# An adjacency pass that adds up in PSUM: pair sums in five banks, copied out by ScalarE, with the weighted one-hots as bf16 thirds from VectorE

## The chip, the cores and the metric

The kernel runs on one core of one Trainium2 chip. The metric is the device time of one execution in microseconds, lower is better; three runs of the kernel before gave a median of 9933.13 us (9930.52 to 9941.49).

## The reference, cut to what matters

Four graph layers over the same graph of 3125 nodes with 48 features and 100000 edges. The change touches how the graph itself is brought into a form that the layers read. The two middle layers are powers of an adjacency matrix, once counted and once weighted:

```
m = segment_sum(w[:, None] * h[row], col)        # layer 1: w from degrees, 5 steps
agg = segment_sum(f[src] * edge_weight[:, None], dst)   # layer 2: 10 steps
```

Layer 0 (attention, four rounds) and layer 3 (one message pass by relation) read sorted edge records and one-hot matrices.

## The kernel before, in words

**Sorting (`sort_edges`, L79 to L624).** Nodes are cut into 25 blocks of 128, so an edge belongs to one of 625 block pairs (source block, destination block). Edges are sorted by pair into tiles of 128 edges, one edge to a partition; each pair has at least one tile, and each source block's tiles are filled up to a multiple of four. There is room for T = 1488 tiles in NG = 372 groups of G = 4. With the inputs used here the 625 pairs need 1080 tiles (270 groups: 44 tiles for most source blocks); the last 102 groups hold no edge and are worked through all the same. A tile's record in DRAM (`REC`) has the numbers of its edge in columns CW to GIDX: cutoff, weight, norm, lane within the source block (SL), lane within the destination block (DL), index. They come from the tile `meta`, which VectorE fills at L272 to L291. The block ends with a loop (L354 to L368) that marks for every tile which pair it belongs to.

**Tables (`tile_tables`, L652 to L717).** VectorE alone works out, on one partition, where each tile's sum belongs (`row_at`), and whether a tile goes on with the pair of the tile ahead (`keep`).

**Adjacency (`adjacency`, L720 to L885).** For each tile a 128x128 matrix of counts and one of weights is made as a product of one-hot matrices, and added to the pair's place in `acc` (128 partitions, 2 x 50 x 128 numbers, two source blocks' rows). A group passes through:
- SyncE: loads the records (L769), and stores the turned one-hots to `OHT` in DRAM (L773), four groups later.
- VectorE: `hots` makes source one-hots and destination one-hots, two tiles at a time, four `tensor_tensor` in a group (L835); `rows` (L859) loads four numbers of `row_at` into registers; `add_up` (L869 to L881) adds each tile's two products into `acc`, one `scalar_tensor_tensor` of 128x256 a tile (L879), two groups behind. The order by hand is at L884: an addition between every two one-hot instructions.
- ScalarE: widens the source one-hots to fp32 (L786), scales the destination one-hots by the weight (L791, four in a group), copies the turned one-hots out of PSUM (L799).
- TensorE: eight transposes (L810, L811), four bf16 products (L820), four fp32 products (L822) in a group.
- GpSimd: clears `acc` at the start (L746), waits for the end of each source block, and sends its row of 3.2 MB to `ADJ` (L759).

The records, one-hots and semaphores have six slots (`laps(..., SLOTS)`), so a stage is at most five groups ahead of what frees its slot.

**After it** come the start of the nodes, gate and attention passes that read `OHT`, two `propagate` calls that read `ADJ` (their GpSimd queue also sends norm, lanes and index on to `REC2`), and the relation pass. Each stage ends in a barrier of all engines.

Of the kernel before, what the change touches and what calls it, by code (L numbers as in the profile page):

```python
# [42 lines left out]
CW, W, NORM, SL, DL, GIDX = 50, 51, 52, 53, 54, 55  # L43
GATES = 56
RW = GATES + H
META = GATES - CW
# [11 lines left out]
ROW = 2 * P * NB  # L58
HOT = 3
# [19 lines left out]
def sort_edges(nc, mem, io):  # L79
# [11 lines left out]
    with ExitStack() as ctx:  # L91
# [31 lines left out]
        turn = sb("turn", [EP, ET], F32)  # L123
# [11 lines left out]
        base = sb("base", [NB, NB], F32)  # L135
        earlier = sb("earlier", [NB, NB], F32)
        ones_n = sb("ones_n", [NB, P], BF16)
        iota_t = sb("iota_t", [NB, T], F16)
        ended = sb("ended", [NB, 2, T], BF16)
        fill2 = sb("fill2", [P, T2 // 8, META - 2], F32)  # L140
# [23 lines left out]
        s_pair = sem("s_pair")  # L164

# [8 lines left out]
        with nc.Block() as block:  # L174
            @block.sync
            def _(sp):
# [13 lines left out]
                sp.wait_ge(s_filled, 16 * (T // FR) + 128)  # L190

            @block.gpsimd
            def _(pool):
# [13 lines left out]
                nc.gpsimd.memset(fill2[:, :, DL - NORM:DL - NORM + 1], -1.0).then_inc(s_fill, 1)  # L207

            @block.scalar
            def _(act):  # L210
                act.wait_ge(s_turn, 1)
                nc.scalar.activation(sine, turn[:], ACT.Sin, scale=SIN_SCALE).then_inc(s_sine, 1)
# [50 lines left out]
            def _(dve):  # L263
# [18 lines left out]
                ch.step(v.tensor_scalar(turn[:], wt[:], 1.0 / 12, None, ALU.mult))  # L282
                ch.step(v.tensor_copy(tmp_i[:], turn[:]))
                ch.step(v.tensor_copy(sine, tmp_i[:]))
                ch.step(v.tensor_tensor(turn[:], turn[:], sine, ALU.subtract))
                v.tensor_scalar(turn[:], turn[:], -1.0, 1.0, ALU.max, ALU.min).then_inc(s_turn, 1)
                ch.step(v.tensor_copy(meta[:, :, W - CW], wt[:]))
                dve.wait_ge(s_sine, 1)
                ch.step(v.tensor_tensor(turn[:], sine, sine, ALU.mult))
                ch.step(v.tensor_scalar(sine, turn[:], -1.0, 1.0, ALU.mult, ALU.add))  # L290
                ch.step(v.scalar_tensor_tensor(meta[:, :, 0], wt[:], 6.0, sine, ALU.is_lt, ALU.mult))  # L291
                dve.wait_ge(s_const, 5)
# [43 lines left out]
                ch.step(v.tensor_scalar(ends[:], ends[:], before[:, 0:1], None, ALU.add))  # L336
                ch.step(v.tensor_tensor(base[:], ends[:], tiles[:], ALU.subtract))
# [87 lines left out]
        with nc.Block() as block:  # L425
# [120 lines left out]
            def _(dve):  # L546
# [22 lines left out]
                def ranks(n, slot, first):  # L569
# [6 lines left out]
                    v.tensor_copy(rec[:, slot, :, CW:GATES], meta[:, cols]).then_inc(s_meta, 1)  # L576
# [75 lines left out]
def tile_tables(nc, mem):  # L652


    for name, shape, dt in (("where", [1, NG * WHERE], I32), ("row_at", [1, NG * G], I32), ("spot", [1, T2], I32), ("goes_on", [P, NG], F32),
                            ("fresh", [P, NG], F32), ("last", [1, NB], I32)):
        mem[name] = nc.alloc_sbuf_tensor("m_" + name, shape, dt)
    with ExitStack() as ctx:
# [3 lines left out]
        odd = sb("odd", [1, T])  # L662
        odd_i = sb("odd_i", [1, T], I32)
# [13 lines left out]
        with nc.Block() as block:  # L677
            @block.vector
            def _(dve):
                v = nc.vector  # L680
                ch = Chain(dve, s_tab)
                ch.note(v.memset(mem["keep"][:, 0:1], 0.0))
                ch.note(v.tensor_tensor(mem["keep"][:, 1:T], mem["pair"][:, 1:T], mem["pair"][:, 0:T - 1],
                                        ALU.is_equal))


# [8 lines left out]
                ch.note(v.tensor_copy(odd_i[:], mem["sblk_t"][0:1, :]))  # L695
                ch.step(v.scalar_tensor_tensor(dblk[:], mem["sblk_t"][0:1, :], -float(NB), pair, ALU.mult, ALU.add))

                ch.note(v.tensor_scalar(sblk[:], mem["sblk_t"][0:1, :], 1.0, float(KEEP), ALU.max, ALU.mult))
                ch.step(v.tensor_scalar(odd_i[:], odd_i[:], 1, None, ALU.bitwise_and))
                ch.step(v.tensor_copy(odd[:], odd_i[:]))  # L700
                row_at = mem["row_at"][:].rearrange("o (g j) -> o g j", j=G)
                ch.step(v.scalar_tensor_tensor(odd[:], odd[:], float(NB), dblk[:], ALU.mult, ALU.add))
# [17 lines left out]
def adjacency(nc, mem):  # L720


    SLOTS = 6
    SUMS = 3
    with ExitStack() as ctx:
        room = Room(nc, ctx, "a_")
        rec = room.sb("rec", [P, SLOTS, G, META])
# [1596 lines left out]
```

## Time and profile before

| what | us |
|---|---|
| median of three runs | 9933.13 |
| span of the profiled execution | 10065.2 |
| sorting, 0 to 1490 | 1490 |
| tables, 1490 to 1536 | 46 |
| adjacency, 1536 to 2928 | 1392 |
| start of nodes and gate pass, 2928 to 3680 | 752 |
| attention, four rounds, 3680 to 7240 | 3560 |
| propagation, twice, 7240 to 8745 | 1505 |
| relation pass and end, 8745 to 10065 | 1320 |

The profiled execution is 132 us (1.3%) longer than the median of the runs without a profile. Over the whole span PE is busy 71%, VectorE (DVE) 60%, GpSimd (POOL) 47%, ScalarE (ACT) 37%. These averages mix stages with different limits; a row of a group of instructions gives its busy time, the mean duration of one, and the idle time of the engine ahead of it with what ended that idle time.

### The profile page before, as it was taken

The numbers are of one execution on the slowest core, as the hardware profiler recorded it, in microseconds if no ns is written. First come the engines' busy times: TensorE is split into PE (matmuls) and PEld (weight loads), VectorE is DVE, ScalarE is ACT, GpSimd is POOL, SyncE is SP. The second block draws the span as 40 slices with busy tenths as digits, with TensorE's granted clock in tenths as the row PEclk, the third lists the DMA queues.
The fourth block names the chain that finished last, engine by engine and source line by source line (L and its number), as shares of the span: only waits on it lengthen the run. The fifth ranks groups of instructions, "written<-read, shape, count | busy, mean of one in ns | idle before, by whom it ended". The sixth has DMA issues, their size and how long they took to land. (4 is left out here: it accounts for less than half of the span.)

```text
span 10065.2 us, 316920 instructions
## 1 busy us (share of the span) xinstructions
PE 7153.0 (71%) x106494; PEld 5756.9 (57%) x106495; DVE 6009.4 (60%) x18492; ACT 3716.3 (37%) x12956; POOL 4708.2 (47%) x6247
## 2 busy tenths in 40 slices
PE   2888865766657849976994998599578788833323
PEld 1555544555547749975994898499434344433323
DVE  6555558888867778997997899799700100011112
ACT  3222216777753326753662676377300000000000
POOL 0777770000016625542551554255267476556665
PEclk9999998888879979987996999799799899855555
DMA  8222224555439949965992997499488899611112
GB/s 330 60 61 61 62 52 162 192 186 188 136 103 308 310 137 255 263 178 147 261 261 65 262 263 205 121 262 263 128 333 334 322 365 364 236 29 18 18 18 19
DMA packets 1841808, 1846.73 MB, mean 183 GB/s; under 512 B 1462965, under 2 KB 1477717, under 8 KB 1796469
## 3 DMA queue, kind: packets, MB, share of 16 engines
q1 hardware_dynamic: 1727618, 1668.62, 54.0%
q0 software_dynamic: 112016, 153.10, 5.9%
q10 hardware_dynamic: 2016, 22.94, 0.6%
q8 instruction: 94, 1.54, 0.1%
q14 instruction: 64, 0.52, 0.0%
HBM read 1481.79 MB, written 360.62 MB: 183 GB/s over the span
## 5 line engine op out<-in xcount | busy, mean ns | idle before, releaser
L1649 POOL TENSOR_TENSOR s_rest<-s_msg 128x196 f32<-128x196 f32 x1488 | 762.6, 512 | 1881.7 <-ACT s_msg L1631 1819.4
L1239 PE MATMUL s_gotd<-m_table_d,s_hot 128*128 x17856 | 1363.2, 205 | 207.3 <-DMA s_hot<-OHT 195.2
L1631 ACT ACTIVATE s_msg<-s_gotd,s_es 128x49 f32<-128x49 f32 x5952 | 1304.4, 303 | 48.3 <-ACT s_es L1624 0.2
L1239 PE MATMUL s_gotq<-m_table_s,s_hot 128*128 x17856 | 1280.0, 185 | 7.1 <-issue 6.9
L1239 PEld LDWEIGHTS s_gotd<-m_table_d,s_hot 128*128 128x128 bf16 x17856 | 989.1, 96 | 291.4 <-DMA s_hot<-OHT 196.6
L1916 POOL DMA_INDIRECT REC<-m_sums x800 | 957.1, 1196 | 353.5 <-issue 346.8
L463 POOL DMA_INDIRECT REC<-rec,place x800 | 960.9, 1201 | 260.5 <-issue 228.5
L2195 POOL DMA_INDIRECT l_row<-H,l_rec x816 | 786.6, 964 | 501.3 <-issue 252.7
L1682 DVE TENSOR_REDUCE s_tops<-s_mt 128x512 f32 (+1 forms) x1488 | 1013.6, 681 | 6.5 <-PE s_mt L1592 6.3
L1949 PE MATMUL p_acc<-p_row,p_feats 128*64 128x512 f32 (+1 forms) x4032 | 900.2, 570 | 160.3 <-DMA p_row<-ADJ 157.3
L1239 PEld LDWEIGHTS s_gotq<-m_table_s,s_hot 128*128 128x128 bf16 x17856 | 992.1, 97 | 5.9 <-issue 5.9
L1253 PE MATMUL l_sums<-l_msg,l_oh 128*128 128x49 f32 x1632 | 373.4, 378 | 817.6 <-issue 798.2
L1253 PEld LDWEIGHTS l_sums<-l_msg,l_oh 128*128 128x128 f32 x1632 | 379.3, 321 | 813.1 <-issue 812.8
L1592 PE MATMUL s_mt<-m_ident_bf,s_raw 128*128 128x128 bf16 x5952 | 823.3, 219 | 4.3 <-issue 4.2
L1591 PE MATMUL s_mt<-s_hot,m_apart 128*128 128x128 bf16 x5952 | 823.0, 218 | 2.9 <-issue 1.7
L1656 POOL TENSOR_TENSOR s_least<-s_rest 128x196 bf16<-128x196 f32 x1488 | 762.9, 513 | 116.7
L1949 PEld LDWEIGHTS p_acc<-p_row,p_feats 128*64 128x64 f32 x4032 | 385.3, 140 | 654.1 <-issue 430.8
L879 DVE SCALAR_TENSOR_TENSOR a_acc<-a_acc,m_keep,a_sums 128x256 f32 x1488 | 706.1, 475 | 64.3 <-issue 49.4
L822 PE MATMUL a_sums<-a_hd_weighted,a_hs_wide 128*128 128x128 f32 x2976 | 662.0, 350 | 0.0
L1612 PE MATMUL s_sums<-s_msg,s_hot 128*128 128x49 bf16 x5952 | 621.0, 186 | 48.8 <-issue 41.1
L1612 PE MATMUL s_sums<-s_least,s_hot 128*128 128x49 bf16 x5952 | 620.6, 184 | 4.1 <-issue 4.1
L1612 PE MATMUL s_sums<-s_rest,s_hot 128*128 128x49 bf16 x5952 | 622.2, 186 | 1.7 <-issue 1.6
(422 smaller groups left out, 18333.1 us busy)
## 6 DMA issues: line engine op xcount, KB each, us to landing
s_hot<-OHT SPq DMA_DIRECT2D x1488, 384.0 KB
p_row<-ADJ SPq DMA_DIRECT2D x288, 1600.0 KB
s_rec<-REC SPq DMA_DIRECT2D x1488, 98.0 KB
OHT<-a_turned SPq DMA_DIRECT2D x372, 384.0 KB
g_hot<-OHT SPq DMA_DIRECT2D x372, 384.0 KB
ADJ<-a_acc POOLq DMA_DIRECT2D x25, 3200.0 KB
REC<-fill SPq DMA_DIRECT2D x124, 624.0 KB, 10.2
g_rec<-REC SPq DMA_DIRECT2D x372, 108.0 KB
```

The costliest lines, as they stand in the source:

```text
L463: nc.gpsimd.indirect_dma_start(out=mem["REC"], out_offset=bass.IndirectOffsetOnAxis(ap=place[:, b, j:j + 1], axis=0), in_=rec[:, b, j], in ...
L1239: last = nc.tensor.matmul(out, hot, table[k][:, bass.ds(at, w)], start=(k == 0), stop=(k == 2))
L1591: nc.tensor.matmul(mt[:, j], mem["apart"][:], hot[:, b, j, 1], start=True, stop=False)
L1592: last = nc.tensor.matmul(mt[:, j], upper(raw[:, b % KEPT, j:j + 1]).to_broadcast([P, P]), mem["ident_bf"][:], start=False, stop=True)
L1612: last = nc.tensor.matmul(sums[:, 0:SW], hot[:, b, j, 2], thirds[k], start=(j == 0 and k == 0), stop=(j == G - 1 and k == 2))
L1631: last = nc.scalar.activation(msg[:, b % KEPT, j], gotd[b % KEPT][:, j, SW:2 * SW], ACT.Copy, scale=es[:, b % 2, j:j + 1])
L1649: nc.gpsimd.tensor_tensor(rest[:, b % KEPT].rearrange("p g w -> p (g w)"), msg[:, b % KEPT].rearrange("p g w -> p (g w)"), upper(msg[:, b ...
L1656: nc.gpsimd.tensor_tensor(least[:, b % KEPT].rearrange("p g w -> p (g w)"), rest[:, b % KEPT].rearrange("p g w -> p (g w)"), upper(rest[:, ...
L1682: v.tensor_reduce(tops[:, bass.ds(n, 1)], mt[:].rearrange("p j e -> p (j e)"), X, ALU.max).then_inc(s_top, 1)
L1916: nc.gpsimd.indirect_dma_start(out=mem["REC2"], out_offset=bass.IndirectOffsetOnAxis(ap=places_of[b][:, t:t + 1], axis=0), in_=numbers_of[ ...
L1949: last = nc.tensor.matmul(acc[odd * SIDE:(odd + 1) * SIDE, q, 0:n * P].rearrange("w (c e) -> w c e", e=P), feats[:, s], source.rearrange(" ...
L2195: nc.gpsimd.indirect_dma_start(out=row[:, b, j], out_offset=None, in_=table, in_offset=bass.IndirectOffsetOnAxis(ap=rec[:, b, j, GIDX - NO ...
```

## The change

- `sort_edges`: `meta` has eight columns instead of six. The weight is stored as three numbers, each exact in bf16 (its bf16 value, the bf16 value of the rest, the rest of that); norm and index move behind DL, and the record in `REC` keeps its width. The running ends of the pairs' tiles are written to DRAM and loaded back onto one partition (`pair_end`) by SyncE. Some tiles share memory with others.
- `tile_tables`: `keep` and `row_at` go; `pair_at` comes, for each tile the start of its PSUM bank, and for a group's last tile also the number of its pair.
- `adjacency`: the counts and weights of a pair's tiles add up in one of five PSUM banks (pair k in bank k mod 5), both products of a tile in bf16: one matmul for the counts, three for the weight's thirds. ScalarE waits for the end of each pair by its number in `pair_end`, copies the bank's 256 columns into `acc`, waits for that, and writes zeros to the bank. It also starts the DMA of each row, which GpSimd did. VectorE makes all one-hots with one `tensor_scalar` a tile and kind: two for the plain ones, three for the weighted ones, with two scalars from the record each; it also copies the turned one-hots out of PSUM. `acc` needs no clearing and no addition.
- `propagate` and `relation_pass` take the columns at their new places.

```diff
@@ sort_edges
-                ch.step(v.tensor_copy(meta[:, :, W - CW], wt[:]))
...
+                third, less = tmp_i[:].bitcast(BF16)[:, 0:ET], turn
+                ch.step(v.tensor_copy(third, wt[:]))
+                ch.step(v.tensor_copy(meta[:, :, W - CW], third))
+                ch.step(v.tensor_tensor(less, wt[:], third, ALU.subtract))
+                ch.step(v.tensor_copy(third, less))
+                ch.step(v.tensor_copy(meta[:, :, W - CW + 1], third))
+                ch.step(v.tensor_tensor(meta[:, :, W - CW + 2], less, third, ALU.subtract))
...
+                v.tensor_copy(ends_i[:], ends[:]).then_inc(s_ends, 1)
...
+                sp.wait_ge(s_ends, 1)
+                sp.dma_start(mem["PAIR_END"].rearrange("(s d) -> s d", d=NB), ends_i[:]).then_inc(s_ends_out, 16)
+                sp.wait_ge(s_ends_out, 16)
+                sp.dma_start(mem["pair_end"][:], mem["PAIR_END"].rearrange("(o k) -> o k", o=1)).then_inc(s_ends_out, 16)
+                sp.wait_ge(s_ends_out, 32)
@@ tile_tables
+                fives = sblk[:]
+                ch.step(v.tensor_scalar(fives, dblk[:], float(BANKS), None, ALU.is_ge))
+                for k in range(2, NB // BANKS):
+                    ch.step(v.scalar_tensor_tensor(fives, dblk[:], float(k * BANKS), fives, ALU.is_ge, ALU.add))
+                ch.step(v.scalar_tensor_tensor(fives, fives, -float(BANKS), dblk[:], ALU.mult, ALU.add))
+                ch.step(v.tensor_copy(bank_i[:], fives))
...
@@ adjacency, ScalarE (widen, weighted, take_turned removed)
+                    for d in range(NB):
...
+                        at = place(half * NB + d)
+                        act.wait_ge(s_sums, act.snap(ended[d % 5] & 2047).with_bounds(min_val=0, max_val=T))
+                        act.sem_inc(s_tick, 1)
+                        nc.scalar.copy(acc[:, :, half * NB + d], flat[:, at:at + 2 * P].rearrange("p (h c) -> p h c", h=2)
+                                       ).then_inc(s_taken, 1)
+                        act.wait_ge(s_taken, i * (2 * NB) + (half * NB + d + 1))
+                        nc.scalar.copy(flat[:, at:at + 2 * P], blank[:]).then_inc(s_free, 1)
...
+                    nc.scalar.dma_start(whole[bass.ds(i * 2 + half, 1)].rearrange("s p h d c -> (s p) h d c"),
+                                        acc[:, :, half * NB:(half + 1) * NB]).then_inc(s_row[half], 16)
@@ adjacency, TensorE
+                    pe.wait_ge(s_thirds, n + 1)
+                    pe.wait_ge(s_free, pairs)
...
                     for j in range(G):
-                        nc.tensor.matmul(sums[b % SUMS][:, j, 0:P], turned[:, b, j, 2], hd[:, b, j], start=True,
-                                         stop=True)
-                        last = nc.tensor.matmul(sums[b % SUMS][:, j, P:2 * P], hs_wide[:, b % 2, j],
-                                                hd_weighted[:, b % 2, j], start=True, stop=True)
-                    last.then_inc(s_sums, 1)
+                        nc.tensor.matmul(flat[:, bass.ds(spots[j], P)], turned[:, b, j, 2], hd[:, b, j], start=False,
+                                         stop=False, skip_group_check=True)
+                        for k in range(PARTS):
+                            last = nc.tensor.matmul(flat[:, bass.ds(spots[j] + P, P)], thirds[:, b, j, k], hd[:, b, j],
+                                                    start=False, stop=False, skip_group_check=True)
+                        last.then_inc(s_sums, 1)
...
-                laps(pe, [(turn, 0), (products, 0)], SLOTS)
+                laps(pe, [(turn, 0), (places, 1), (products, 1)], SLOTS)
@@ adjacency, VectorE (hots, rows, add_up removed)
+                def lanes(out, b, j, at):
+                    return v.tensor_scalar(out, mem["iota_bf"][:], rec[:, b, j, at - CW:at - CW + 1], None, ALU.is_equal)
+
+                def hots(n, b, lap):
+                    dve.wait_ge(s_rec[b], 16 * lap + 16)
+                    if past(lap, 1):
+                        dve.wait_ge(s_sums, G * (n - (SLOTS - 1)))
+                        dve.wait_ge(s_oht[b], 16 * lap)
+                    for j in range(G):
+                        lanes(turned[:, b, j, 2], b, j, SL)
+                        last = lanes(hd[:, b, j], b, j, DL)
+                    last.then_inc(s_hot, 1)
+
+                def weighted(n, b, lap):
+                    for j in range(G):
+                        for k in range(PARTS):
+                            last = v.tensor_scalar(thirds[:, b, j, k], mem["iota_bf"][:],
+                                                   rec[:, b, j, SL - CW:SL - CW + 1],
+                                                   rec[:, b, j, W - CW + k:W - CW + k + 1], ALU.is_equal, ALU.mult)
+                    last.then_inc(s_thirds, 1)
+
+                def take_turned(n, b, lap):
+                    dve.wait_ge(s_ptr, n + 1)
+                    v.tensor_copy(turned[:, b, :, 0:2], ptr[b % 2][:]).then_inc(s_turned, 1)
+
+                laps(dve, [(hots, 0), (take_turned, 1), (weighted, 0)], SLOTS)
```

## Rows read from the trace of the kernel before

**Rows 1.** Stage: us; PE, PEld, DVE, ACT, POOL busy (count); PE clock, DMA share, GB/s
```profile
1536.00:2928.00 1392.00, 947.51 (x7440) 790.27 (x7440) 1147.58 (x2976) 1027.25 (x2232) 28.95 (x28) 0.85 0.51 169
```
**Rows 2.** Groups of instructions, adjacency stage: count, busy us, mean ns, idle before
```profile
L879 DVE SCALAR_TENSOR_TENSOR a_acc<-a_acc,m_keep,a_sums 128x256 f32 x1488 | 706.1, 475 | 64.3 <-issue 49.4 <-POOLq L750 5.6 <-DVE a_acc L879 1.5
L835 DVE TENSOR_TENSOR a_turned<-m_iota,a_rec 128x256 bf16<-128x256 f32 x744 | 313.3, 421 | 179.7 <-issue 137.4 <-PE a_sums L822 28.5 <-DMA a_rec<-REC 12.1
L799 ACT COPY a_turned<-a_ptr 128x1024 bf16<-128x1024 bf16 x372 | 367.6, 989 | 0.0
```
**Rows 3.** Waits in the adjacency stage: who for whom, us, times, longest
```profile
POOL ADJ L759 <- DVE a_acc L879: 992.6, 25, 41.9
PE a_ptr L810 <- DVE a_hd L835: 279.3, 267, 88.0
```
**Rows 4.** VectorE in one group: start, duration, idle time ahead in brackets
```profile
2087.34 0.48 DVE L879 SCALAR_TENSOR_TENSOR a_acc<-a_acc,m_keep,a_sums 128x256 f32 x1 [0.16 <-issue]
2087.74 0.42 DVE L835 TENSOR_TENSOR a_turned<-m_iota,a_rec 128x256 bf16<-128x256 f32 x1
2088.07 0.47 DVE L879 SCALAR_TENSOR_TENSOR a_acc<-a_acc,m_keep,a_sums 128x256 f32 x1
...
2090.74 0.42 DVE L835 TENSOR_TENSOR a_turned<-m_iota,a_rec 128x256 bf16<-128x256 f32 x1 [0.75 <-issue]
```
**Rows 5.** Two short VectorE instructions without a scalar from memory, in order of time
```profile
2.06 0.22 DVE L646 TENSOR_SCALAR m_lower<-diff 128x128 f32<-128x128 f32 x1
2.20 0.22 DVE L647 TENSOR_SCALAR m_apart<-diff 128x128 bf16<-128x128 f32 x1
```
**Rows 6.** Two back to back (in order of time), each with one scalar from memory
```profile
218.14 1.11 DVE L357 TENSOR_SCALAR ended<-iota_t,ends 25x1488 bf16<-25x1488 f16 x2
```
**Rows 7.** VectorE's groups at the end of sorting, with and without such a scalar
```profile
L357 DVE TENSOR_SCALAR ended<-iota_t,ends 25x1488 bf16<-25x1488 f16 x25 | 14.8, 595 | 15.2 <-PE pair_ps L250 15.2
L336 DVE TENSOR_SCALAR ends<-ends,before 25x25 f32<-25x25 f32 x1 | 0.2, 227 | 0.0
L321 DVE TENSOR_SCALAR tiles<-tiles 25x25 f32<-25x25 f32 x1 | 0.2, 168 | 0.0
```
**Rows 8.** A VectorE copy out of PSUM, in order of time
```profile
253.24 0.69 DVE L367 COPY m_pair<-pair_ps 128x512 f32<-128x512 f32 x1
```
**Rows 9.** ScalarE's copies: out of PSUM in propagation, and SBUF to SBUF
```profile
L1983 ACT COPY p_feats<-p_back 128x240 f32<-128x240 f32 x16 | 5.8, 364 | 1.4 <-PE p_back L1968 1.3
L786 ACT CAST a_hs_wide<-a_turned 128x512 f32<-128x512 bf16 x372 | 229.8, 618 | 151.7 <-DVE a_turned L835 143.1 <-PE a_sums L822 4.6
```
**Rows 10.** ScalarE waiting for its own instruction, in attention
```profile
5002.06 0.20 ACT L1624 ACTIVATE s_es<-s_diff 128x4 f32<-128x4 f32 x1 [0.42 <-DVE s_diff L1694]
5002.30 0.88 ACT L1631 ACTIVATE s_msg<-s_gotd,s_es 128x49 f32<-128x49 f32 x4
```
**Rows 11.** TensorE at the lower clock in the adjacency stage
```profile
2086.19 0.31 PE L810 MATMUL a_ptr<-m_ident_bf,a_hd 128*128 128x128 bf16 x1
2086.29 0.31 PE L811 MATMUL a_ptr<-m_ident_bf,a_turned 128*128 128x128 bf16 x1
```
**Rows 12.** VectorE fills the records' numbers; the start of the next block
```profile
31.73 0.58 DVE L283 CAST m_place<-turn 125x800 int32<-125x800 f32 x1
...
37.20 1.57 DVE L291 SCALAR_TENSOR_TENSOR m_meta<-wt,src_i 125x800 f32<-125x800 f32 x1
256.81 0.64 DVE L368 COPY m_sblk_t<-sb_ps 128x464 f32<-128x464 f32 x1
257.94 2.88 POOL L449 MEMSET rec<- 125x3328 f32 x1 [251.28 <-POOLq L174]
```
**Rows 13.** VectorE's groups in the tables
```profile
L702 DVE SCALAR_TENSOR_TENSOR odd<-odd,dblk_t 1x1488 f32<-1x1488 f32 x1 | 1.7, 1697 | 0.0
L705 DVE TENSOR_SCALAR sblk_c<-m_sblk_t 1x1488 f32<-1x1488 f32 x1 | 0.9, 924 | 0.0
```
**Rows 14.** VectorE's first addition
```profile
1547.46 0.48 DVE L879 SCALAR_TENSOR_TENSOR a_acc<-a_acc,m_keep,a_sums 128x256 f32 x1 [5.61 <-POOLq L750]
```

More of the change, by code:

```diff
@@ L58 @@
 ROW = 2 * P * NB
+BANKS = 5
+AT_BITS = 12
 HOT = 3
@@ L795, in take_turned @@
-                def take_turned(n, b, lap):
-                    act.wait_ge(s_ptr, n + 1)
-                    if past(lap, 1):
-                        act.wait_ge(s_oht[b], 16 * lap)
-                    nc.scalar.copy(turned[:, b, :, 0:2], ptr[b % 2][:]).then_inc(s_turned, 1)
-                laps(act, [(widen, 0), (weighted, 0), (take_turned, 1)], SLOTS)
+                act.wait_ge(s_blank, 1)
+                for k in range(BANKS):
+                    nc.scalar.copy(flat[:, place(k):place(k) + 2 * P], blank[:]).then_inc(s_free, 1)
@@ new lines, in block_row @@
+                def block_row(i, half, first=False):
+                    if not first:
+                        act.wait_ge(s_row[half], 16 * i)
+                    ended = []
+                    for d in range(NB):
+                        if d % 5 == 0:
+                            _, values = nc.values_load_multi_w_load_instructions(
+                                mem["pair_end"][0:1, bass.ds(i * (2 * NB) + (half * NB + d), 5)], engines=[act.engine],
+                                min_val=1, max_val=T,
+                                skip_runtime_bounds_check_because="each pair has a tile, and all have T at most")
+                            ended = list(values)
+                        at = place(half * NB + d)
[5 more added lines that the diff above has]
+                        nc.scalar.copy(flat[:, at:at + 2 * P], blank[:]).then_inc(s_free, 1)
+                    whole = mem["ADJ"].rearrange("(s p h d) c -> s p h d c", s=NB, p=P, h=2)
+                    nc.scalar.dma_start(whole[bass.ds(i * 2 + half, 1)].rearrange("s p h d c -> (s p) h d c"),
+                                        acc[:, :, half * NB:(half + 1) * NB]).then_inc(s_row[half], 16)
@@ L803, in _ @@
+                for half in range(2):
+                    block_row(0, half, first=True)
+                with act.Fori(1, NB // 2) as i:
+                    for half in range(2):
+                        block_row(i, half)
+                block_row(NB // 2, 0)
+                for half in range(2):
+                    act.wait_ge(s_row[half], 16 * len(range(half, NB, 2)))
             @block.tensor
             def _(pe):
+                at = {}
                 def turn(n, b, lap):
@@ L851, in destinations @@
-                def destinations(pair):
-                    def stage(n, b, lap):
-                        last = hots(hd[:, b, 2 * pair:2 * pair + 2], b, pair, DL)
-                        if pair == 1:
-                            last.then_inc(s_hot, 1)
-                    return stage
-                def rows(n, b, lap):
-                    _, values = nc.values_load_multi_w_load_instructions(
-                        mem["row_at"][0:1, bass.ds(n * G, G)], engines=[dve.engine], min_val=0,
-                        max_val=KEEP * NB + 2 * NB - 1,
-                        skip_runtime_bounds_check_because="tile_tables works them out from blocks below NB")
-                    kept = dve.snap((values[0] >> 6) & 31).with_bounds(min_val=1, max_val=NB)
-                    first_row = dve.snap(values[0] - kept * KEEP)
-                    at[b] = kept, [v.with_bounds(min_val=0, max_val=2 * NB - 1) for v in (first_row, *values[1:])]
```

169 lines of the change are left out of this document (61 added, 108 removed).

## The prediction

> **What bounds the kernel now.** The view by stages comes first: the adjacency stage takes 1392 us for 372 groups, 3.74 us a group, and VectorE is the busiest engine in it (1148 us), ahead of ScalarE (1027) and TensorE (948), with GpSimd nearly idle and the DMA engines at half load [rows 1]. The groups of instructions then show what VectorE does: four additions and four one-hot instructions a group [rows 2]. The waits show the others behind it: GpSimd waits 993 us for the additions, TensorE's transposes 279 us for the destination one-hots [rows 3]. VectorE itself idles most often for "issue" (137 us ahead of the first one-hot, 49 us ahead of an addition), against 12 us for the records' DMA [rows 2]: that is its own sequencer loading and splitting four numbers for register addresses. In order of time one group reads: addition to one-hot 0.40 us, one-hot to addition 0.33 us, four times, so 2.92 us, and 0.75 + 0.16 us idle around the register work [rows 4] (less in other groups, 3.74 on average). So VectorE's queue is the bound of the stage, and what the change is worth is read from VectorE's queue after it. No other stage's work changes but for small parts of sorting and tables.
>
> **Prices on VectorE.** The duration of a row is not what an instruction costs in a queue: the next one starts before the row ends. The two short ones without a scalar from memory start 0.14 us apart with a duration of 0.22 [rows 5]. A row of 1488 numbers has 595 ns [rows 7], and two in a row end after 1.11 us [rows 6], so they start 0.515 us apart, 0.08 less than the duration. A scalar read from memory costs 59 ns (227 against 168 for the same shape) [rows 7]; the addition, which has one, agrees (475 - 421 = 54) [rows 2], and it isn't hidden: 0.40 against 0.33 in the queue [rows 4]. f32 in `tensor_scalar` runs at about 0.52 ns an element ((924 - 150)/1488 [rows 13], with 150 fixed from rows 5: 220 - 128 x 0.52), 16 bits at 0.26 ((595 - 208)/1488, 208 being 150 + 58) [rows 7].
>
> **VectorE after, a group.**
> - Eight plain one-hots: one scalar, 128 numbers from bf16 to bf16: 0.128 fixed in the queue (0.515 - 0.387) + 128 x 0.26 ns = 0.16 us, so 1.29 us.
> - Twelve weighted ones: two scalars. No row has two. Below, the second comes free with the first: 0.16 us, 1.93 in all. Above, it costs another 59 ns: 0.22 us, 2.64. I take 0.22, since the first was paid in full beside everything else.
> - The copy out of PSUM, moved from ScalarE, where it took 989 ns [rows 2]: 1024 bf16 numbers. The nearest row copies 512 f32 numbers, the same bytes, in 0.69 us, 1.04 ns a number [rows 8]. If two 16-bit numbers go in place of one word, 0.69 - 0.08 = 0.61 us; if each costs 1.04, 1.15 us. I take 0.61, since from SBUF 16 bits halve the time a number (0.26 against 0.52).
> - Register loads leave VectorE; waits that count laps stay. 0.1 us, bounds 0 and 0.3 (most of what idles now is the loads).
>
> The Trainium skill (VectorE: DVE Perf Modes, "Why PSUM operands drop a tier") caps an operand in PSUM at the mode that takes two 16-bit numbers a cycle, which would be the 0.61; no row here shows a bf16 copy out of PSUM by VectorE.
>
> Sum: 1.29 + 2.64 + 0.61 + 0.1 = **4.64 us a group against 3.74**, so +0.90 x 372 = +335 us. Work is not saved by count: eight instructions of 0.33 to 0.40 give way to twenty of 0.16 to 0.22 and a copy. The 102 groups without edges pay the same.
>
> **What lies beside it.**
> - ScalarE, a pair: copy out of PSUM 0.38 (364 ns for 240 numbers and 0.8 ns for each more; 0.8 from 989 for 1024) [rows 2, 9]; its wait for itself 0.04 (5002.06 + 0.20 to 5002.30) [rows 10]; zeros back 0.41 (618 ns for 512, less 256 x 0.8) [rows 9]; register work 0.1 to 0.3. About 1.0 us, 625 us for 625 pairs, beside 1726. Behind its waits are queued only its own later pairs and the rows' DMAs, and TensorE waits for it. It matters in bursts: some 15 pairs of one tile follow one another in each source block, four to a group, 4.0 us against 4.64. I replayed the queues pair by pair with these inputs' tile counts: the stage stays at VectorE's time up to 1.5 us a pair, because VectorE may run two groups ahead.
> - TensorE: four fp32 products go, twelve bf16 ones come: 24 at 0.10 us at the lower clock (start to start) [rows 11] is 2.5 us, and if the register loads cost it what they cost VectorE (0.9), 3.4, still under 4.64. Its turned one-hots of group n come ahead of the products of n - 1, which wait for banks; two groups of slack lie between that and VectorE's copy.
> - SyncE: load and store each group as before, no later than VectorE. Its two added DMAs of the pairs' ends wait for numbers that are ready before VectorE's loop over the tiles begins, and for the fills; that loop hides them, and without it they would cost the few microseconds of two small transfers one after the other. Nothing.
> - GpSimd: loses 25 DMA issues and the clearing of `acc`, behind which the first addition waited 5.6 us [rows 14]: -6 us. The rows' DMAs on ScalarE's queue move the same bytes, at half load [rows 1].
> - Sorting: six instructions of 125x800 come: 0.6 us a plain one, up to 1.6 a strided one [rows 12]: 5 to 8 us, take 6. The removed copy lay beside the sine. This is on the path: GpSimd's next block starts after VectorE's last copy [rows 12].
> - Tables: three big additions and comparisons at 1.7 more, some at 0.9 less [rows 13]: +3 us.
> - `propagate` loads 8 instead of 6 numbers an edge, always one chunk ahead of GpSimd's indirect DMAs, which hide it: nothing.
>
> Together +335 - 6 + 6 + 3 = +338. The profiled execution spans 10065 us, 132 more than the median of the runs; the differences are laid on the median: 9933 + 338 = **10271, say 10270 us**.
>
> **Rivals.**
> 1. The second scalar is free. 3.93 us a group, +0.19 x 372 + 3 = +74: 10007. For it: both scalars come from one record, next to one another. Against: one costs 59 ns on its own. 0.35.
> 2. The copy takes 1.15 us: +201 more. With two paid scalars 10472, with one 10208. For it: rows 8 as they stand. Against: the halving at 16 bits. 0.11 together.
> 3. **Faster.** An instruction's scalar is read while the one ahead still runs, when all twenty are alike and need no wait; the price is then that of rows 5 less the narrower numbers, 0.07 + 0.033 = 0.104. The place is the run of twenty in VectorE's queue: 2.08 + 0.61 + 0.1 = 2.79 us a group; the replay gives 1058 us with ScalarE at 1.0 a pair, since its bursts then show, so -334 + 3: about 9600. It decides from 0.15 us an instruction down (20 x 0.15 + 0.71 = 3.71). Against: rows 6 are two alike with no wait between them, and pay. 0.08. The Trainium skill (VectorE: DVE Perf Modes, "The TRN2 errata") gives 58 cycles and a quarter cycle a number, 94 ns here, and 0.66 us for the copy: 2.6 us a group and near 9520; the same section says that this falls short of measured durations, and the row of 227 ns for 25 numbers bears that out.
> 4. ScalarE's pair takes 2.5 us (register waits that drain its queue): the replay gives some 2030 us, 10570. Against: rows 10. 0.02.
> 5. Gains and costs cancel: 0.17 us less in a group than rival 1. 0.03.
>
> That leaves 0.41 for the forecast. About 0.2% (20 us) is what a measurement of this kernel can tell from no change. **Chances:** faster 0.08, same 0.03, slower 0.89. **Range:** down to rival 1 with no register time (3.83 a group, 9970), so 9975, up to the forecast with 0.3 idle (10345) and part of rival 2: 9975 to 10400. The forecast alone would have 10230 to 10350.
>
> **What the profile would show.** VectorE's plain one-hots at about 241 ns, weighted ones at 241 or 300, starting 0.16 and 0.16 or 0.22 apart; the copy at 0.69 or 1.23; the stage at about 1725 us with VectorE busy nearly throughout; ScalarE idle for products of TensorE, TensorE for the thirds. If VectorE idles for the turned one-hots or for slots, and TensorE for ScalarE's zeros, rival 4 holds. One-hots 0.10 apart would make the sign wrong.

## The result, and the profile after

| | time, us (median, lowest to highest, runs) | adjacency stage, us | the stage divided by its 372 groups, us |
|---|---|---|---|
| before | 9931.8 (9927.1 to 9941.5, 4) | 1392 | 3.74 |
| after | 10266.4 (10260.2 to 10274.2, 4) | 1721 | 4.63 |

The change makes the kernel slower: ratio 1.0341, interval 1.0329 to 1.0353, +334.5 us. Forecast were 10270 and +338. The profiled execution of after spans 10263.6 us, as its timed runs do. The profile of before has a span 133 us longer than its median. That excess lies in the relation pass at the end, whose products take 1186 us there and 1048 us in after (first to last of L1253, L1263 in after). Up to the first of them after lies 336.7 us behind, close to the measured +334.5. The stage's length is read in all kernels from GpSimd's first clearing in it to GpSimd's first instruction of the next one (1542.96 to 3263.91 in after).

The stage of after by busy time, with the same columns as [rows 1]:

```profile
1543.00:3262.00 1719.00, 1011.59 (x8927) 825.30 (x8928) 1702.09 (x7812) 452.42 (x1255) 1.45 (x3) 0.59 0.41 138
```

VectorE is busy for 1702 of 1719 us, where it was busy for 1148 of 1392 [rows 1]. ScalarE fell from 1027 to 452, and TensorE's granted clock from 0.85 to 0.59. The groups of instructions in the stage (count, busy us, mean ns, idle time before) say what fills VectorE:

```profile
L885 DVE TENSOR_SCALAR a_thirds<-m_iota_bf,a_rec 128x128 bf16<-128x128 bf16 x4464 | 1023.4, 301 | 0.0
L856 PE MATMUL a_ring<-a_hd,a_turned 128*128 128x128 bf16 x1488 | 435.7, 293 | 57.3 <-issue 54.3 <-ACT a_ring L813 2.0 <-DVE a_thirds L885 0.8
L870 DVE TENSOR_SCALAR a_turned<-m_iota_bf,a_rec 128x128 bf16<-128x128 bf16 x1488 | 358.1, 241 | 16.0 <-DMA a_rec<-REC 16.0
```

The destination one-hots (`a_hd`) have the same 358.1 us and 241 ns as the source ones. The durations are the two that the prediction named, 241 and 300 ns. VectorE's idle time is 16 us, in two waits for records, the longer one 13 us; the 137 and 49 us of "issue" ahead of its one-hots and additions [rows 2] are gone. TensorE waited 2 us for ScalarE's banks and 0.8 for the thirds. The waits turn the same way round (who for whom, us, times, longest):

```profile
PE a_ptr L836 <- DVE a_hd L870: 736.9, 372, 90.6
ACT a_acc L810 <- PE a_ring L859: 732.1, 278, 26.1
```

TensorE waits for VectorE once in each of the 372 groups, 737 us in all, against 279 us before [rows 3]. ScalarE waits for TensorE, which had waited for VectorE. In order of time, one group on VectorE (compare [rows 4]):

```profile
2212.18 0.24 DVE L870 TENSOR_SCALAR a_turned<-m_iota_bf,a_rec 128x128 bf16<-128x128 bf16 x1
2212.35 0.24 DVE L870 TENSOR_SCALAR a_hd<-m_iota_bf,a_rec 128x128 bf16<-128x128 bf16 x1
...
2213.48 0.67 DVE L892 COPY a_turned<-a_ptr 128x1024 bf16<-128x1024 bf16 x1
2214.09 2.75 DVE L885 TENSOR_SCALAR a_thirds<-m_iota_bf,a_rec 128x128 bf16<-128x128 bf16 x12
2216.76 0.23 DVE L870 TENSOR_SCALAR a_turned<-m_iota_bf,a_rec 128x128 bf16<-128x128 bf16 x1
```

Eight plain one-hots in 1.30 us (0.163 apart), the copy in 0.61, twelve weighted ones in 2.67 (0.222 apart): 4.58 us from group to group. Nothing stands between them.

### The profile page after: what moved, and what is told of

Same layout as the page of the kernel before. It is cut to its first block and busy times, and to the rows that moved or that the text cites. A ratio compares the mean times of both kernels' runs of the same rounds, so it can differ in the third digit from the quotient of the medians.

```text
span 10263.6 us, 324752 instructions
## 1 busy us (share of the span) xinstructions
PE 7240.1 (71%) x107982; PEld 5781.0 (56%) x107983; DVE 6595.1 (64%) x23334; ACT 3138.9 (31%) x11980; POOL 4678.6 (46%) x6222
## 5 line engine op out<-in xcount | busy, mean ns | idle before, releaser
L885 DVE TENSOR_SCALAR a_thirds<-m_iota_bf,a_rec 128x128 bf16<-128x128 bf16 x4464 | 1023.4, 301 | 0.0
L1263 PE MATMUL l_sums<-l_msg,l_oh 128*128 128x49 f32 x1632 | 395.4, 417 | 657.3 <-DVEq L2241 657.3
L836 PE MATMUL a_ptr<-m_ident_bf,a_hd 128*128 128x128 bf16 x1488 | 315.9, 289 | 736.9 <-DVE a_hd L870 736.9
L1263 PEld LDWEIGHTS l_sums<-l_msg,l_oh 128*128 128x128 f32 x1632 | 363.5, 328 | 690.5 <-issue 690.5
L836 PEld LDWEIGHTS a_ptr<-m_ident_bf,a_hd 128*128 128x128 bf16 x1488 | 186.6, 130 | 832.8 <-DVE a_hd L870 708.1
```

The costliest lines, as they stand in the source:

```text
L885: last = v.tensor_scalar(thirds[:, b, j, k], mem["iota_bf"][:], rec[:, b, j, SL - CW:SL - CW + 1], rec[:, b, j, W - CW + k:W - CW + k + 1] ...
```

## The experiments

Twelve kernels ran, each beside the kernel before. All but one start from the changed kernel. The stage is the adjacency stage.

| run | time, us | ratio to before, interval | stage, us |
|---|---|---|---|
| one_scalar | 9995.3 | 1.0070 (1.0053 to 1.0087) | 1452 |
| first_scalar | 10087.6 | 1.0159 (1.0142 to 1.0176) | 1541 |
| act_blanks | 10296.1 | 1.0377 (1.0359 to 1.0394) | 1752 |
| act_blanks5 | 10518.4 | 1.0597 (1.0581 to 1.0613) | 1979 |
| no_thirds | 9654.3 | 0.9721 (0.9705 to 0.9738) | 1108 |
| before_fixed | 9748.9 | 0.9818 (0.9802 to 0.9835) | 1214 |
| pool_thirds | 9987.5 | 1.0063 (1.0046 to 1.0080) | 1449 |
| broadcast | 9863.6 | 0.9935 (0.9919 to 0.9952) | 1314 |
| broadcast16 | 9927.9 | 1.0003 (0.9993 to 1.0012) | 1384 |
| pairs16 | 9642.5 | 0.9709 (0.9693 to 0.9725) | 1097 |
| pairs16_ahead | 9615.6 | 0.9689 (0.9676 to 0.9702) | 1076 |
| pairs16_later | 9627.1 | 0.9693 (0.9679 to 0.9706) | 1075 |

### The price of a number read from memory: one_scalar, first_scalar

```diff
 def weighted(n, b, lap):
+    dve.wait_ge(s_hot, n + 1)
...
-            last = v.tensor_scalar(thirds[:, b, j, k], mem["iota_bf"][:],
-                                   rec[:, b, j, SL - CW:SL - CW + 1],
-                                   rec[:, b, j, W - CW + k:W - CW + k + 1], ALU.is_equal, ALU.mult)
+            last = v.tensor_scalar(thirds[:, b, j, k], turned[:, b, j, 2],
+                                   rec[:, b, j, W - CW + k:W - CW + k + 1], None, ALU.mult)
```

> The changed kernel, but the weighted thirds are made from the source one-hot that is already there, times one number from memory, instead of from the lane numbers with two (one comparison, one product). Theory (VectorE's queue bounds the stage, and each number read from memory costs 0.059 us there): 12 instructions a group lose 0.059 us, 0.71 us x 372 groups = -263 us; the thirds start 0.163 us apart instead of 0.222, the stage takes 1456 us instead of 1719, the kernel 10003. Rival (the weighted ones are dearer for their second operation or for another reason, or the stage waits for something else): no change, 10266; if the price is half the second operation's and half the number's, -130.

Measured 9995.3, 271 us less than after; forecast 263. In order of time in one_scalar:

```profile
2212.24 0.67 DVE L892 COPY a_turned<-a_ptr 128x1024 bf16<-128x1024 bf16 x1
2212.84 2.02 DVE L886 TENSOR_SCALAR a_thirds<-a_turned,a_rec 128x128 bf16<-128x128 bf16 x12
2214.79 0.24 DVE L870 TENSOR_SCALAR a_turned<-m_iota_bf,a_rec 128x128 bf16<-128x128 bf16 x1
```

The twelve take 1.95 us instead of 2.67, so 0.162 each, as a plain one-hot. This run alone can't say whether the second number or the second operation was dear, as both went. The next one takes a number away and leaves the operation:

```diff
-return v.tensor_scalar(out, mem["iota_bf"][:], rec[:, b, j, at - CW:at - CW + 1], None, ALU.is_equal)
+return v.tensor_scalar(out, mem["iota_bf"][:], 5.0, None, ALU.is_equal)
```

> The changed kernel, but the eight plain one-hots of a group compare with a constant instead of the record's number; which source and destination an edge has is left out, so the sums are of a fixed row. Theory (a number read from memory costs VectorE's queue 0.059 us, also in a run of like instructions): the plain one-hots start 0.104 us apart instead of 0.163, 8 x 0.059 x 372 = -176 us, the kernel 10090. Rival 3 of the prediction (in a run of like instructions the number is read while the one ahead still works): no change, 10266.

Measured 10087.6, 179 us less; forecast 176. The plain one-hots now have 180 ns and start 0.10 apart (in order of time):

```profile
2212.71 0.18 DVE L870 TENSOR_SCALAR a_hd<-m_iota_bf 128x128 bf16<-128x128 bf16 x1
2212.81 0.18 DVE L870 TENSOR_SCALAR a_turned<-m_iota_bf 128x128 bf16<-128x128 bf16 x1
```

So one number costs 0.06 us in the queue in a run of like instructions without a wait: rival 3 falls, and its price of 0.104 us is that of an instruction with no number to read. 180, 241 and 301 ns for none, one and two numbers are equal steps, which leaves nothing for the second operation.

### ScalarE's pairs: act_blanks, act_blanks5

```diff
+for k in range(3):
+    nc.scalar.copy(more[:, k], blank[:])
 nc.scalar.copy(flat[:, at:at + 2 * P], blank[:]).then_inc(s_free, 1)
```

> The changed kernel, but ScalarE copies the zeros three more times for each pair into buffers that nobody reads, so that a pair costs it about 1.9 us (0.75 to 0.85 plus 3 x 0.37) instead of 0.8. Theory (ScalarE lies beside VectorE's 4.62 us a group, with two groups of slack, and shows only in its bursts): replayed queue by queue the stage grows by 20 to 45 us, the kernel takes 10285 to 10310. Rival (ScalarE's pairs are on the path, TensorE waits for each bank): +1.1 us x 625 pairs = +690 us, 10950.

> As the run with three more copies of zeros a pair on ScalarE, but five more, so that a pair costs it about 2.6 us. Theory (ScalarE shows in its bursts only, with VectorE two groups ahead): the replay of the queues gives +360 us over the changed kernel, 10630; the corner lies near 1.8 us a pair. Rival (its time is hidden on average, 625 pairs x 2.6 = 1625 us being less than the stage's 1719): no more than the 30 us of three copies, 10300.

Measured +30 us with three copies and +252 with five. In order of time with five, a pair, and then the waits there over the whole stage:

```profile
2216.71 0.36 ACT L811 COPY a_acc<-a_ring 128x256 f32<-128x256 f32 x1
2217.10 1.63 ACT L815 COPY a_more<-a_blank 128x256 f32<-128x256 f32 x5
2218.64 0.36 ACT L816 COPY a_ring<-a_blank 128x256 f32<-128x256 f32 x1
2218.95 0.36 ACT L811 COPY a_acc<-a_ring 128x256 f32<-128x256 f32 x1
```
```profile
PE a_ring L859 <- ACT a_ring L816: 573.6, 138, 7.1
DVE a_turned L895 <- PE a_ptr L840: 251.6, 76, 4.6
```

A copy more costs ScalarE 0.31 us, not the 0.40 of its mean duration, so the pair took 2.24 us (1.63 with three) and not 2.6. Both rivals fall: on the path, 625 pairs x 1.5 us more would be +960, and hidden on average five copies would show no more than three. The chain is the one of rival 4: TensorE waits for banks, its transposes stand behind, and VectorE waits for those, for 252 us in all, which is what the kernel lost. With three copies the same wait of VectorE is 30 us, again what the kernel lost. So the corner, the time of a pair from which the stage grows, lies below the 1.63 us of the first run, and not at the 1.8 us that the replay gave. The replay's size is off too: the expectation had +360 us at 2.6 us a pair, and a straight line from its corner to that gives about +200 us at 2.24 (an estimate), where the run shows 252. In after a pair costs 0.71 us in a burst:

```profile
2348.01 0.37 ACT L810 COPY a_acc<-a_ring 128x256 f32<-128x256 f32 x1 [1.43 <-PE a_ring L859]
2348.41 0.38 ACT L813 COPY a_ring<-a_blank 128x256 f32<-128x256 f32 x1
2348.72 0.37 ACT L810 COPY a_acc<-a_ring 128x256 f32<-128x256 f32 x1
```

### How far down VectorE is the bound: no_thirds

```diff
-    PARTS = 3
+    PARTS = 1
```

> The changed kernel with one third of the weight only: the second and third parts of the weights are left out, on VectorE (8 instructions fewer a group) and on TensorE (8 products fewer), so the weighted sums are those of weights rounded to bf16. Theory: VectorE 8 x 0.163 + 4 x 0.222 + 0.61 + 0.06 = 2.87 us a group, the stage 1067 us, 650 less, the kernel 9615; that is still VectorE's, since ScalarE at 0.8 us a pair needs under that. Rival (a second bound lies close under 4.62 us a group, in ScalarE's bursts, TensorE's register work or the chain from one-hot to turned one-hot): the stage stays above 1250 us, the kernel above 9800.

Measured 9654.3, 612 us less than after; forecast 651. The stage takes 1108 us and not 1067. The missing 41 us stand in its waits:

```profile
PE a_ring L856 <- ACT a_ring L813: 87.1, 85, 5.0
DVE a_turned L870 <- DMA a_rec<-REC: 34.6, 17, 14.8
DVE a_turned L870 <- PE a_ring L859: 16.5, 10, 1.8
DVE a_turned L892 <- PE a_ptr L837: 12.2, 13, 3.2
```

VectorE waits 63 us in all (14 to 16 of them once, at the start, as in after). At 2.87 us a group the next bounds begin to show, for the records as well as for ScalarE's banks.

### What VectorE's register loads cost before: before_fixed

```diff
-place = acc[:, :, bass.ds(places[j], 1)].rearrange("p h k c -> p h (k c)")
+place = fixed[:, :, j]
...
-laps(dve, [(rows, 2), (sources(0), 0), (add_up(0), 2), (sources(1), 0), (add_up(1), 2),
+laps(dve, [(sources(0), 0), (add_up(0), 2), (sources(1), 0), (add_up(1), 2),
```

> The kernel before, but its additions go to four fixed places, so that VectorE loads no register for them; that the sums reach their rows of the adjacency is left out, all other work stays. Theory (of the 3.74 us a group 2.92 were work and the rest VectorE's sequencer): 3.0 us a group, -275 us, the kernel 9655. Rival (ScalarE at 2.76 and TensorE at 2.55 us a group, and the wait of one addition for the one before, take over): -100 us or less, above 9830.

Measured 9748.9, 181 us less than before; forecast 275. Two lines of its groups (count, busy us, mean ns, idle before):

```profile
L880 DVE SCALAR_TENSOR_TENSOR a_fixed<-a_fixed,m_keep,a_sums 128x256 f32<-128x256 f32 x1419 | 672.8, 474 | 31.5 <-PE a_sums L824 25.2 <-POOL a_acc L748 6.2
L837 DVE TENSOR_TENSOR a_turned<-m_iota,a_rec 128x256 bf16<-128x256 f32 x712 | 298.1, 419 | 84.5 <-DMA a_rec<-REC 79.6
```

Between theory and rival. The "issue" idle time (187 us together [rows 2]) went, and the queue's own work is 2.90 us a group, 1079 us. But the stage takes 1214: the waits for the records' DMA grew from 12 us [rows 2] to 80, and the additions now wait 25 us for TensorE's sums, a wait that their row of [rows 2] doesn't name. The step that failed in this expectation is that all the time beyond VectorE's own work was put down to the loads.

### Moving a third of the thirds: pool_thirds

```diff
+for j in range(G):
+    last = nc.gpsimd.tensor_scalar(thirds[:, b, j, 2], mem["iota_bf"][:],
+                                   rec[:, b, j, SL - CW:SL - CW + 1],
+                                   rec[:, b, j, W - CW + 2:W - CW + 3], ALU.is_equal, ALU.mult)
...
-        for k in range(PARTS):
+        for k in range(2):
```

> The changed kernel, but GpSimd, idle in this stage, makes the last third of each tile's weighted one-hots (four of twelve a group), TensorE and SyncE wait for both. Theory (only VectorE's queue counts): 4 x 0.222 = 0.89 us a group less, -331 us, the kernel 9935, if GpSimd's own take less than 0.93 us each. Rival A (GpSimd is slower than that): the stage follows GpSimd, over 1719 us if one takes over 1.15 us. Rival B (the two engines disturb one another in memory): VectorE's instructions show longer than 241 and 301 ns, and less than half of the 331 us comes.

Measured 9987.5, 279 us less; forecast 331. Groups up to 2612 us:

```profile
L778 POOL TENSOR_SCALAR a_thirds<-m_iota_bf,a_rec 128x128 bf16<-128x128 bf16 x1099 | 948.8, 876 | 116.2 <-DMA a_rec<-REC 70.0 <-PE a_ring L874 46.2
L900 DVE TENSOR_SCALAR a_thirds<-m_iota_bf,a_rec 128x128 bf16<-128x128 bf16 x2184 | 516.5, 324 | 0.0
L885 DVE TENSOR_SCALAR a_hd<-m_iota_bf,a_rec 128x128 bf16<-128x128 bf16 x1094 | 303.0, 277 | 0.0
```

GpSimd takes 876 ns for what VectorE does in 0.22 us, just under the 0.93 at which it would have been the bound. VectorE's instructions are longer than in after (324 against 301, 277 against 241): the mechanism of rival B is there. VectorE waits 17 us in the stage, as in after (16), so the longer instructions are all that is missing, 52 us of 331 and not half. The longest weighted one-hot of VectorE takes 458 ns (310 in after) and the shortest of GpSimd 787, so none of VectorE's stood still for a whole instruction of GpSimd. That the two share a resource is inferred from this, not shown by a run of its own. The Trainium skill (GPSIMD Engine Reference, the table of its specifications, "SBUF interfaces") says that GpSimd's way to memory is shared with VectorE's, with contention when VectorE runs a mode with two ports or reads two inputs from SBUF. The lengthening agrees with that, and in which mode VectorE ran no run here shows.

### Fewer and longer instructions: broadcast, broadcast16, pairs16

```diff
-for j in range(G):
-    lanes(turned[:, b, j, 2], b, j, SL)
-    last = lanes(hd[:, b, j], b, j, DL)
+lane = mem["iota"][:].unsqueeze(1).to_broadcast([P, G, P])
+v.tensor_tensor(turned[:, b, :, 2], lane, scalars(SL), ALU.is_equal)
+v.tensor_tensor(hd[:, b], lane, scalars(DL), ALU.is_equal).then_inc(s_hot, 1)
...
+v.tensor_tensor(thirds[:, b], turned[:, b, :, 2].unsqueeze(2).to_broadcast([P, G, PARTS, P]),
+                rec[:, b, :, W - CW:W - CW + PARTS].unsqueeze(3).to_broadcast([P, G, PARTS, P]),
+                ALU.mult).then_inc(s_thirds, 1)
```

> The changed kernel with the same sums, but VectorE makes the one-hots of four tiles with one tensor_tensor each for sources and destinations (the lane numbers against the record's number, broadcast) and all twelve thirds with one tensor_tensor (source one-hots times weights, broadcast): three instructions instead of twenty. Theory (VectorE's queue is the bound, numbers at 1.04 ns each plus 0.07 us): 2 x 0.60 + 1.67 + 0.61 for the copy = 3.48 us a group instead of 4.62, the stage 1300 us, the kernel 9845, faster than before the change. Rival (another engine or the chain of waits through TensorE takes over near 3.7 us a group): 9930 or more.

Measured 9863.6, forecast 9845: 65 us faster than before the change, which is only 0.65% but clear of the interval. In order of time, one group of broadcast:

```profile
2212.72 0.68 DVE L881 TENSOR_TENSOR a_turned<-m_iota,a_rec 128x512 bf16<-128x512 f32 x1
2213.32 0.68 DVE L882 TENSOR_TENSOR a_hd<-m_iota,a_rec 128x512 bf16<-128x512 f32 x1
2213.93 0.68 DVE L892 COPY a_turned<-a_ptr 128x1024 bf16<-128x1024 bf16 x1
2214.53 1.75 DVE L886 TENSOR_TENSOR a_thirds<-a_turned,a_rec 128x1536 bf16<-128x1536 bf16 x1
2216.19 0.68 DVE L881 TENSOR_TENSOR a_turned<-m_iota,a_rec 128x512 bf16<-128x512 f32 x1
```

3.47 us a group, where 3.48 was forecast. The same sums in the same banks, and the kernel is faster than before: what made the change slow is how the one-hots are made on VectorE, not the sums in PSUM. The next two runs narrow the records' numbers to bf16 first. In pairs16 each stands twice, side by side:

```diff
+v.tensor_copy(rec16[:, b], rec[:, b].unsqueeze(3).to_broadcast([P, G, GATES - CW, 2]))
...
+def scalars(at):
+    return rec16[:, b, :, at - CW:at - CW + 1].to_broadcast([P, G, P // 2, 2])
+lane = twos(mem["iota_bf"][:].unsqueeze(1).to_broadcast([P, G, P]))
+v.tensor_tensor(twos(turned[:, b, :, 2]), lane, scalars(SL), ALU.is_equal)
```

> As the run broadcast, but the numbers of the records are first narrowed to bf16 and written twice side by side, so that every operand of the comparisons and of the products is 16 bits and steps by one in its innermost dimension (four products instructions, one a tile). Theory (VectorE takes two 16-bit numbers a cycle then, 0.52 ns each): 0.1 + 2 x 0.34 + 4 x 0.27 + 0.61 = 2.47 us a group; the stage would be 920 us by VectorE alone and 950 to 1050 with ScalarE's and TensorE's bursts, the kernel 9500 to 9600. Rival (1.04 ns a number as before): 0.1 + 1.2 + 4 x 0.47 + 0.61 = 3.79 us a group, the stage 1430 us, the kernel 9980.

> As the run pairs16, but each narrowed number stands once, so that the broadcast operand has step 0 in its innermost dimension, and one instruction makes all twelve thirds. Theory (only operands that step by one let VectorE take two 16-bit numbers a cycle): 1.04 ns a number, 0.1 + 1.2 + 1.67 + 0.61 = 3.58 us a group, the stage 1350 us, the kernel 9900. Rival (16 bits are enough): 0.1 + 0.68 + 0.87 + 0.61 = 2.26 us a group, the kernel 9640 as pairs16 or faster.

Measured 9642.5 and 9927.9. One group of each in order of time, pairs16 first:

```profile
2212.04 0.42 DVE L889 TENSOR_TENSOR a_turned<-m_iota_bf,a_rec 128x512 bf16<-128x512 bf16 x1
2212.38 0.42 DVE L890 TENSOR_TENSOR a_hd<-m_iota_bf,a_rec 128x512 bf16<-128x512 bf16 x1
2212.72 0.68 DVE L904 COPY a_turned<-a_ptr 128x1024 bf16<-128x1024 bf16 x1
2213.32 1.15 DVE L895 TENSOR_TENSOR a_thirds<-a_turned,a_rec 128x384 bf16<-128x384 bf16 x4
2214.39 0.18 DVE L875 CAST a_rec<-a_rec 128x48 bf16<-128x48 f32 x1
2214.48 0.42 DVE L889 TENSOR_TENSOR a_turned<-m_iota_bf,a_rec 128x512 bf16<-128x512 bf16 x1
```
```profile
2212.84 0.68 DVE L886 TENSOR_TENSOR a_turned<-m_iota_bf,a_rec 128x512 bf16<-128x512 bf16 x1
2213.44 0.68 DVE L887 TENSOR_TENSOR a_hd<-m_iota_bf,a_rec 128x512 bf16<-128x512 bf16 x1
2214.04 0.68 DVE L897 COPY a_turned<-a_ptr 128x1024 bf16<-128x1024 bf16 x1
```

The rows read alike (512 numbers, bf16 from bf16), and take 0.34 us from start to start in one and 0.60 in the other. What differs is the broadcast operand, whose innermost dimension has a step of 1 in one and of 0 in the other. The Trainium skill (VectorE: DVE Perf Modes, "What auto-detection actually checks") asks for 16 bits and a step of one in every tensor before this engine takes two numbers a cycle in an instruction with two sources; both runs agree. A group takes 2.44 us in pairs16 (2.47 forecast), and 3.55 in broadcast16 (3.58 forecast), where the narrowing is paid for nothing. The kernel broadcast16 comes out 28 us above its forecast of 9900: VectorE waits 53 us for records in it, against 17 in broadcast. Yet the stage takes 1097 us and not 372 x 2.44 = 908, and the kernel 43 us more than the upper end of what was expected.

### What bounds the stage next: pairs16_ahead, pairs16_later

The waits in the stage of pairs16:

```profile
DVE a_rec L875 <- DMA a_rec<-REC: 128.6, 26, 17.0
PE a_ring L857 <- ACT a_ring L814: 128.0, 126, 5.0
DVE a_turned L904 <- PE a_ptr L838: 42.8, 49, 2.5
```

```diff
+# in GpSimd's block, with AHEAD = 12 slots of rec
+def load(n, b, lap):
+    if past(lap, 1):
+        pool.wait_ge(s_narrow, n - (AHEAD - 1))
+    nc.gpsimd.dma_start(rec[:, b], numbers(mem, n, CW, GATES)).then_inc(s_rec[b], 16)
...
-laps(sp, [(load, 0), (store_turned, 4)], SLOTS)
+laps(sp, [(store_turned, 0)], SLOTS)
```

> As the run pairs16, but GpSimd's queue issues the loads of the records, each as soon as its slot is narrowed, with twelve slots for the records instead of six, so that a load is issued some 12 groups ahead instead of some 4, and not behind a store. Theory (with VectorE at 2.44 us a group the records land late when a row of the adjacency is written: 129 us of waits in 26 places, and VectorE's own work is 908 us of a stage of 1095): the waits for records go, the stage takes 970 to 1020 us, the kernel 9520 to 9570. Rival (TensorE's waits for banks, 128 us, hold the same places): the stage stays above 1060 us, the kernel above 9610.

Measured 9615.6, 27 us less than pairs16, not 75 to 125; its waits:

```profile
PE a_ring L860 <- ACT a_ring L817: 179.7, 156, 4.3
DVE a_turned L907 <- PE a_ptr L841: 123.4, 159, 4.5
PE a_ptr L840 <- DVE a_hd L893: 113.9, 19, 108.9
...
DVE a_rec L878 <- DMA a_rec<-REC: 21.2, 1, 21.2
```

The waits for records went as the theory said (one is left, the first load), but 80 us came back as VectorE's wait for TensorE's transposes, so the rival had most of it. The third line shows that the order of the engines has turned: after the first group (108.9 us) TensorE waits only 5 us more for VectorE's one-hots, where it waited 737 us in after. The stage now goes at TensorE's pace, and what holds that up are ScalarE's banks (180 us) and "issue" ahead of the products (113 us), the place where TensorE's registers are loaded. The last run lets the products fall one group further behind:

```diff
-laps(pe, [(turn, 0), (places, 1), (products, 1)], SLOTS)
+laps(pe, [(turn, 0), (places, 2), (products, 2)], SLOTS)
```

> As the run pairs16_ahead, but TensorE turns the one-hots of two groups before it makes the products of the first of them (products two groups behind instead of one), so that VectorE's copy of a group's turned one-hots does not stand behind products that wait for ScalarE's banks. Theory (in pairs16_ahead VectorE waits 123 us in 159 places for TensorE's transposes, which stand in TensorE's queue behind such products, 180 us of waits for banks): most of these go, the stage takes 980 to 1020 us instead of 1075, the kernel 9520 to 9560. Rival (ScalarE's burst itself is the limit there, and the wait only moves to VectorE's one-hots, for slots): the stage stays above 1050 us, the kernel above 9590.

```profile
PE a_ring L860 <- ACT a_ring L817: 153.7, 141, 4.3
DVE a_turned L907 <- PE a_ptr L841: 123.0, 142, 4.5
```

Measured 9627.1. Nothing came of it: the stage is the same, the wait is the same 123 us, and the two times don't differ by more than their intervals. The theory falls.

In order of time, two of ScalarE's copies in a burst of pairs, with four more pairs between them, from the same run:

```profile
2233.19 0.37 ACT L814 COPY a_acc<-a_ring 128x256 f32<-128x256 f32 x1 [1.03 <-PE a_ring L863]
...
2237.51 0.37 ACT L814 COPY a_acc<-a_ring 128x256 f32<-128x256 f32 x1 [0.71 <-PE a_ring L863]
```

Of the rival one half, that the wait would move to VectorE's one-hots, didn't happen. The other half, that ScalarE's burst is the limit, has the sums for it: in a burst of pairs of one tile ScalarE needs 4 x 0.71 = 2.84 us a group, more than VectorE's 2.44. But it isn't the whole: in the middle of the burst above ScalarE itself stands idle for 1.03 and 0.71 us until TensorE's next products are done, the second time after five pairs in a row, as many as there are banks. So TensorE waits for banks and ScalarE for products, by turns. Whether a faster pair, more banks or fewer register loads on TensorE would shorten the stage was not tried and stays open.

## Why the prediction was right, point by point

- **The bound.** VectorE's queue before and after: shown by one_scalar, first_scalar, no_thirds and broadcast, whose times follow VectorE's sums to within 8, 3, 39 and 19 us in that order, and by act_blanks, in which ScalarE's time a pair more than doubles for +30 us.
- **Plain one-hots**, 0.16: measured 0.163, duration 241 ns as named.
- **Weighted ones**, 0.22 against a lower bound of 0.16: 0.222. This was the largest choice, with 0.35 on the other side, and it rested on one reason, that the first number is paid in full. one_scalar is what rival 1 would have looked like: 9995 against its 10007.
- **The copy**, 0.61 against 1.15: 0.61 (duration 673 to 691 ns in the runs). Rival 2 falls. Two 16-bit numbers go for one of 32 bits out of PSUM too.
- **Residue**, 0.1: 0.05 (1721/372 = 4.63 a group in the stage, less 4.58 in order of time), and 0.04 of that are the 16 us of waits for records. This term was too high by 0.05 x 372 = 19 us, and the rounding of the others gave 0.04 x 372 = 15 back (4.54 forecast, 4.58 measured): the stage took 1721 us for a forecast of 1726.
- **Start**, -6: VectorE's first one-hot comes 2.4 us after the stage's start, and no wait for a clearing of `acc` is left [rows 14]. But the prediction counts this gain twice. Its 3.74 us are the whole stage before divided by 372, with that wait in them, so the +335 has the gain already. Without the second count the forecast is +344, 9 us off instead of 3: that the total came so near is in part luck.
- **Sorting**, +6: GpSimd's first clearing behind it moved from 257.94 [rows 12] to 264.01, +6.1. But the tables start only 3.8 us later (1493.88 for 1490.10), so 2 of the 6 were absorbed in between; by what isn't shown. The six instructions themselves take 5.7 us (39.02 to 44.73 in after), up to 1.59 us each.
- **Tables**, +3: 49 us for 46.
- **ScalarE's pair**, 1.0 us: 0.71 in a burst. Two terms were too high: the duration was taken for the cost in the queue, where 0.31 counts, and the register work costs nothing within a run of five pairs. It hid either way: VectorE has no wait for TensorE in after. The replay's corner, 1.5 us a pair, isn't contradicted (30 us at 1.63); above it the replay is too flat.
- **TensorE**, 24 x 0.10 and no more than 3.4 us: 2213.62 to about 2216.5 in one group, 2.9 us, then 1.8 us of waiting for VectorE's one-hots. Hidden.
- **SyncE, GpSimd, `propagate`**, nothing: nothing shows.
- **Rival 3** is refuted by first_scalar's 179 us, rival 5 (no change) by the result, rival 4 by the 0.71 us that a pair takes. The chain that rival 4 describes exists all the same, as act_blanks5 shows.

The sum, by stretches: stage +329 (forecast +335 and -6), tables +3, sorting and what follows it +4, together +336, for a measured +334.5.

## What to carry to other kernels

An engine that is already the bound pays for each instruction by its place in the queue, from start to start, and each number that it reads from memory, one to a partition, is part of that: 0.06 us a piece here, so the twenty short instructions with 32 such operands cost 1.9 us a group for those alone. Work of that kind goes into a few long instructions with broadcast operands, in 16 bits, and the broadcast operand written twice side by side so that its innermost step is one: on VectorE 2.44 us a group against 4.58, and in all 9643 us (9616 with the records loaded further ahead) against 9932 before and 10266 after the change. What is taken off the bound is won only down to the next wait, so look at what ends second before pricing a saving: taking VectorE's register loads away was forecast at 275 us and gave 181, and loading the records ahead 75 to 125 and gave 27.

## What the runs showed that was not expected

- The step of the innermost dimension decides whether a bf16 `tensor_tensor` takes 0.66 or 1.17 ns a number from start to start (0.34 and 0.60 us for 512), and neither the row's shape nor its type shows it.
- GpSimd makes a weighted one-hot in 876 ns, four times VectorE's 0.22 us, and lengthens VectorE's own instructions from 241 to 277 and from 301 to 324 ns on average while it does.
- ScalarE's copies of 256 f32 numbers start 0.31 us apart in a run, with a mean duration of 0.36 to 0.40.
- TensorE's mean granted clock was 0.59 of full speed over the stage of after, so mostly at the lower of its two levels (1.2 GHz), after 0.85 before [rows 1], while the engine waited 737 us for one-hots. VectorE never waited for TensorE in that stage, so it cost nothing here.
